# Attention kernel with two feed-forward nets: the second net's portions moved by half a unit, an eviction in three operations, and the smoothing states read earlier

## The chip, the cores and the metric

The kernel runs on one core of a Trainium2 chip. The metric is the device time of one execution in microseconds (us), as the median of several executions. The core has five engines that work side by side and meet at semaphores: TensorE (PE in the rows, with its weight loads as PEld), VectorE (DVE), ScalarE (ACT), GpSimd (POOL) and SyncE (SP), whose instructions here are DMA issues.

## The reference

Four batches of 2048 tokens with 256 features are normalised, and two blocks read the result. All is float32.

```python
xh = x[:, :, :DH]                                  # DH = 128, 8 heads of 16
x1 = layernorm(xh + mha(xh, wq1, ...), g1, be1)
xs = holt(x, 0.1, 0.1)                             # a linear recurrence over the tokens
x2 = layernorm(xs[..., :DH] + mha(xs[..., :DH], wq2, ...), g2, be2)
y = concatenate([x1, x2], -1)
attn = layernorm(y + relu(y @ w_ff1.T + b_ff1) @ w_ff2.T + b_ff2, g_ff, be_ff)
ffn = relu(x @ W1 + b1) @ W2 + b2                  # 256 -> 1024 -> 256, the "second net"
out = x_in + attn + ffn                            # x = layernorm(x_in)
```

## The kernel before

Each batch passes through three stages, and each engine has its own program in which they follow one another: a **prologue** (transposes, the smoothing of `holt`, the projections to keys, queries and values), the **attention**, and the **nets** (the first net, `w_ff`, and the output). In `middle(b)` the prologue of batch b+1 stands between the attention and the nets of batch b.

**The attention** is 16 units (`PAIRED_UNITS`: two attentions, four chunks of 512 queries, two groups of four heads). A unit has 16 key tiles, here called kts, and each kt has two steps, so `STEPS = 32`. A step is one product of keys and queries on TensorE (`scores`, line 1487) and one exponential over 128x1024 on ScalarE (line 746). The scores go to two buffers in turn, so `scores(at)` waits until exponential `at - 2` is done. A kt also has one product with the values (`values`, line 1505), which adds into two PSUM banks `o_banks` over the whole unit; the two banks hold the sums over the two halves of the keys. At the first kt of the next unit `values` waits for `o_read`, that is until VectorE has read both banks. The order of TensorE's instructions is written out by hand in `attention` (lines 1509 to 1527): in each kt two scores, then the values, and between the two scores, in kts named by lists, a piece of other work.

**That other work** is the second net, cut into 8 halves of 256 tokens for a batch (`HALVES`, index `i`). The first layer of a half is 8 portions (`second_hidden`, k = 0 to 7), the second layer 8 more (`second_out_part`; k = 0 to 3 make the first tile of 128 tokens, k = 4 to 7 the second). Before, an even unit 2i has the 8 portions of the first layer of half i, and the odd unit 2i+1 the 8 portions of its second layer. All products of a portion are 48 instructions of line 1270, written into the two PSUM banks `sides`. VectorE takes up each portion of the first layer with `hidden_half` (lines 921 to 927, four operations; `hid2_read` is counted after the second), and portion k + 1 waits for `hid2_read` of portion k. Each tile of the second layer is taken up by `second_tile` (lines 936 and 943).

**The end of a unit.** VectorE's `evict` (lines 864 to 870) reads both `o_banks`, adds them and shuffles the rows. After an odd unit the pair of groups is complete: `second_sums`, two `invert` (the reciprocal, line 887) and `attended` (lines 893 and 895) make `att`, TensorE's `out_projection` multiplies it (line 1270 too, 64 instructions into the same `sides`), and `add_projection` (lines 913 and 915) adds it to `resid`. `check_sums` (899 to 903) is a test of ranges. In the even unit these pieces stand between the first-layer portions on VectorE: `hidden_half` 0, `second_sums`, `hidden_half` 1, `invert(0)`, and so on. `out_projection` stands in kt 9, and waits for `att_ready` and for `hid2_read` of portion 4, which VectorE reads after `attended`. In some odd units VectorE has a layer norm of the next batch (`layer_norm`) or `first_y` between its two `second_tile`.

**The smoothing in the prologue of a later batch ("joint")**: TensorE makes local states, VectorE copies them (`local_states`), then each chunk's state follows from the one before (`next_state` on both engines, lines 1365 and 1026), and each smoothed chunk is finished by `carried` (line 1383). `out_projection` of the last unit follows `carried(2)`, and the transposes (`turned`, line 1337) wait for `out_read`, the end of `add_projection`.

Of the kernel before, what the change touches and what calls it, by code (L numbers as in the profile page):

```python
# [73 lines left out]
HIDDEN_KTS, OUT_KTS, PROJECTION_KT, BEFORE_PROJECTION = [0, 2, 4, 6, 8, 11, 13, 14], [0, 2, 4, 6, 8, 10, 12, 14], 9, 5  # L74
# [139 lines left out]
def build(nc, x, packed, w_ff, w_ffn, out):  # L214
# [8 lines left out]
    with ctx:  # L223
# [71 lines left out]
        def fast_programs():  # L295
# [493 lines left out]
            def vector_program(dve):  # L789
# [71 lines left out]
                def evict(b, n):  # L861
# [3 lines left out]
                    dve.tensor_copy(o_sb[:, n % 2, :], o_banks[1]).then_inc(o_read, 1)  # L865
                    hold(dve, o_read, u + 2)
                    step.settle()
                    step(dve.tensor_tensor(rden[:, :], rden[:, :], o_sb[:, n % 2, :], ALU.add))
                    step.settle()
# [134 lines left out]
                def prologue(b, before=None):  # L1004
# [88 lines left out]
                    if before is not None:  # L1093
                        evict(before, UNITS2 - 1)
                        second_sums()
                        invert(0)
                        local_states()
                        invert(1)
                        next_state(2)
                        attended(before, UNITS2 - 1)  # L1100
                        next_state(3)
                        state_read()
                        check_sums(before, UNITS2 - 1)
                        add_projection(before, UNITS2 - 1)
                        smoothed()
# [54 lines left out]
                def attention(b, next_norm):  # L1160
                    for n in range(UNITS2):
# [3 lines left out]
                        if n % 2 == 0:  # L1165
                            hidden_half(b, i, 0)
                            if n > 0:
                                second_sums()
                            hidden_half(b, i, 1)
                            if n > 0:  # L1170
                                invert(0)
                            hidden_half(b, i, 2)
                            if n > 0:
                                invert(1)
                            hidden_half(b, i, 3)
                            if n > 0:
                                attended(b, n - 1)
                            hidden_half(b, i, 4)
                            if n > 0:
                                add_projection(b, n - 1)  # L1180
                                check_sums(b, n - 1)
                            for k in range(5, HB):
                                hidden_half(b, i, k)
                        else:
# [17 lines left out]
                            second_tile(b, i, 1)  # L1202

# [1331 lines left out]
```

## Time and profile before

| | us |
|---|---|
| median of 3 executions | 2614.68 (2612.33 to 2617.86) |
| the profiled execution, device time | 2602.86 |
| its span | 2601.0 |
| TensorE (PE) busy | 2356.7 (91%) |
| ScalarE busy | 2183.9 (84%) |
| VectorE busy | 1627.0 (63%) |
| exponentials (line 746), busy | 1313.5 + 671.5 |

The span is the time between the first and the last instruction. Busy time is merged over instructions that overlap, so TensorE's 91% counts a time in which a pipelined product is still in flight as busy. The exponentials overlap their neighbours slightly too, which is why 2048 of 1.04 us each make 1985 us.

### The profile page before, as it was taken

Reading aid. Unit: us, or ns where it says so; the run is one execution under the profiler, and the core shown is the slowest. Engines: PE = TensorE matmul, PEld = TensorE weight load, DVE = VectorE, ACT = ScalarE, POOL = GpSimd, SP = SyncE. Lnnn points to the kernel's source line nnn. Section 1 sums busy time; section 2 is a strip of 40 time slices with the busy share of each in tenths; the row PEclk is TensorE's granted clock in tenths of the full one; section 3 lists DMA queues with packets and bytes.
Section 4 is the critical chain, followed back from the end, with each engine's and each line's share of the span. In section 5 each row is a group of like instructions: output and inputs, shape, how many; then the busy total and the mean of one; then the engine's idle time right before and its main releaser. Section 6 shows DMA issues by size and latency. Waiting matters only on the chain.

```text
span 2601.0 us, 134879 instructions
## 1 busy us (share of the span) xinstructions
PE 2356.7 (91%) x62849; PEld 1206.9 (46%) x62849; DVE 1627.0 (63%) x3603; ACT 2183.9 (84%) x2419; POOL 382.2 (15%) x375
## 2 busy tenths in 40 slices
PE   6899899999999989999999999999999999999995
PEld 4344444446644444445654444444565444444454
DVE  5456666667746666665775656666577565566676
ACT  5899999976499999996569999999556999999952
POOL 1100100004410020000440002000054000100053
PEclk9999999999999999998999999999899999999998
DMA  8100210005110030000610002000151000200001
GB/s 223 47 20 24 49 37 12 8 7 125 55 39 20 20 62 12 12 8 7 139 60 20 20 20 62 12 12 8 38 109 51 12 12 24 50 12 12 8 30 42
DMA packets 49946, 100.33 MB, mean 39 GB/s; under 512 B 7888, under 2 KB 32464, under 8 KB 48992
## 3 DMA queue, kind: packets, MB, share of 16 engines
q1 hardware_dynamic: 42880, 76.92, 10.8%
q0 software_dynamic: 6496, 14.69, 3.2%
q8 instruction: 494, 8.09, 1.3%
q14 instruction: 76, 0.62, 0.1%
HBM read 57.45 MB, written 34.08 MB: 35 GB/s over the span
## 4 chain that ended last, share of the span: by engine, by line
ACT 37%; PE 25%; DVE 22%; issue 14%; DMA 1%; POOL 1%; DVEq 0%; SPq 0%; ACTq 0%; POOLq 0%
ACT p_sb L746 24%; ACT area L746 12%; PE slot L1557 5%; PE slot L1505 5%; PE slot L1573 5%; DVE rden L887 4%; DVE hid_one L921 3%; PE slot L1487 2%; PE slot L1270 2%; DVE hid_one L923 2%; PE slot L1392 2%; DVE hid_parts L927 2%; DVE o_sb L893 2%; DVE hid_parts L925 1%; PE slot L1401 1%
## 5 line engine op out<-in xcount | busy, mean ns | idle before, releaser
L746 ACT ACTIVATE p_sb<-slot 128x1024 f32<-128x1024 f32 x1368 | 1313.5, 1038 | 99.9 <-PE slot L1487 88.1
L1487 PE MATMUL slot<-q_st,k_st 50*32 50x512 f16 x16384 | 840.0, 381 | 124.9 <-ACT p_sb L746 76.0
L1505 PE MATMUL slot<-p_sb,v_sb 64*17 64x512 f32 x10944 | 724.9, 593 | 0.1
L746 ACT ACTIVATE area<-slot 128x1024 f32<-128x1024 f32 x680 | 671.5, 1039 | 19.0 <-PE slot L1487 17.6
L1487 PEld LDWEIGHTS slot<-q_st,k_st 50*32 50x32 f16 x16384 | 240.3, 90 | 933.9 <-ACT p_sb L746 614.2
L936 DVE SCALAR_TENSOR_TENSOR second<-slot,second 128x256 f32<-128x256 f32 x128 | 54.3, 424 | 506.9 <-PE slot L1270 504.8
L1505 PE MATMUL slot<-area,v_sb 64*17 64x512 f32 x5440 | 358.3, 589 | 0.5 <-issue 0.5
L1270 PE MATMUL slot<-xt_parts,w_parts 64*32 64x256 f16 x12288 | 217.9, 269 | 7.9 <-issue 3.5
L1270 PE MATMUL slot<-w_parts,hid_parts 64*32 64x256 f16 x12288 | 216.5, 268 | 2.0 <-issue 1.9
L1505 PEld LDWEIGHTS slot<-p_sb,v_sb 64*17 64x17 f32 x10944 | 199.5, 94 | 35.9 <-issue 2.7
L921 DVE TENSOR_SCALAR hid_one<-slot,b_grown 128x256 f32<-128x256 f32 x256 | 123.7, 483 | 120.4 <-PE slot L1270 115.1
L1270 PEld LDWEIGHTS slot<-xt_parts,w_parts 64*32 64x32 f16 x12288 | 163.7, 92 | 67.1 <-DVE hid_one L923 36.5
L1270 PEld LDWEIGHTS slot<-w_parts,hid_parts 64*32 64x32 f16 x12288 | 173.0, 93 | 43.2 <-issue 10.1
L1573 PE MATMUL slot<-wf_parts,p_sb 128*128 128x256 f16 x1536 | 175.0, 273 | 5.3 <-POOL p_sb L620 5.3
L1557 PE MATMUL slot<-area,wf_parts 128*128 128x512 f16 x768 | 170.4, 382 | 2.5 <-DVE area L964 2.5
L600 POOL TENSOR_TENSOR resid<-resid,con 128x1024 f32<-128x1024 f32 x16 | 37.9, 2367 | 877.4 <-DVEq L954 877.4
L620 POOL TENSOR_TENSOR p_sb<-area,p_sb 128x512 f16<-128x512 f32 x128 | 149.9, 1172 | 100.0 <-ACT p_sb L762 94.0
L1573 PEld LDWEIGHTS slot<-wf_parts,p_sb 128*128 128x128 f16 x1536 | 148.9, 98 | 29.9 <-POOL p_sb L620 9.7
L443 POOL DMA_DIRECT2D k_st<-part_dram x48 | 24.4, 514 | 834.5 <-PE slot L1505 833.6
L761 ACT ACTIVATE area<-slot,bf_grown 128x512 f32<-128x512 f32 x128 | 88.0, 687 | 50.1 <-PE slot L1557 45.1
L927 DVE SCALAR_TENSOR_TENSOR hid_parts<-hid_one,hid_parts 128x256 f16<-128x256 f32 x256 | 118.5, 463 | 8.7
L887 DVE RECIPROCAL rden<-den 128x256 f32<-128x256 f32 x64 | 112.1, 1752 | 9.1 <-DVE hid_parts L927 1.0
(125 smaller groups left out, 2205.1 us busy)
## 6 DMA issues: line engine op xcount, KB each, us to landing
part_dram<-p_sb SPq DMA_DIRECT2D x16, 1024.0 KB, 4.1
xn<-x SPq DMA_DIRECT2D x16, 512.0 KB, 5.1
second<-x SPq DMA_DIRECT2D x32, 256.0 KB, 3.4
ffn_dram<-second SPq DMA_DIRECT2D x32, 256.0 KB, 2.3
area<-ffn_dram SPq DMA_DIRECT2D x16, 512.0 KB, 5.1
out<-area SPq DMA_DIRECT2D x15, 512.0 KB, 3.3
k_st<-part_dram SPq DMA_DIRECT2D x24, 256.0 KB, 11.4
k_st<-part_dram POOLq DMA_DIRECT2D x48, 128.0 KB, 3.7
```

The lines of the kernel that those rows point to most:

```text
L620: pool.tensor_tensor(h_lo[:, m, :], h_one[:, m % 2, :], h_hi[:, m, :], ALU.subtract).then_inc(hid_ready, 1)
L746: act.activation(p_ring[n % P_RING], slot[n % 2][:, :], ACT.Exp, scale=0.25 / GROW ** 2).then_inc(exp_done, 1)
L761: act.activation(h_one[:, m % 2, :], bank, ACT.Relu, bias=bf_grown[:, m:m + 1])
L887: step(dve.reciprocal(rden[:, cols], den[:, cols]))
L921: step(dve.tensor_scalar(hid_one[:, :], sides[0][:, cols], b1_grown[:, k:k + 1], None, ALU.add))
L927: dve.scalar_tensor_tensor(hid_lo[:, k, :], hid_one[:, :], 0.0, hid_hi[:, k, :], ALU.max, ALU.subtract).then_inc(hid2_ready, 1)
L936: out = dve.scalar_tensor_tensor(tile, sides[r][:, t * D:(t + 1) * D], 1.0 / (X_GROW * W_GROW * W_GROW), tile, ALU.mult, ALU.add)
L1270: mm = pe.matmul(sides[r][ROW * j:ROW * (j + 1), cols], lhs[rows_, ROW * j:ROW * (j + 1)], rhs[rows_, :], start=start, stop=stop, skip_gro ...
L1487: mm = pe.matmul(slot[n][ROW * r:ROW * (r + 1), k * CHUNK:(k + 1) * CHUNK], k_st[rows_, pair, kt * P + ROW * r:kt * P + ROW * (r + 1)], q_ ...
L1505: mm = pe.matmul(o_banks[r][ROW * j:ROW * j + DK + 1, :], v_sb[rows_, a, kt, GH * g + j, :], p_ring[n % P_RING][rows_, (j % 2) * CHUNK:(j ...
L1557: mm = pe.matmul(slot[m // 2 % 2][:, (m % 2) * CHUNK:(m % 2 + 1) * CHUNK], w[:, k, m * P:(m + 1) * P], src[:, k * CHUNK:(k + 1) * CHUNK], ...
L1573: mm = pe.matmul(bank[:, t * D:(t + 1) * D], src[:, m, t * P:(t + 1) * P], w[:, m, :], start=(m == 0 and r == 0), stop=(m == HB - 1 and r ...
```

## The change

The portions are placed anew, half of each layer in each unit. An even unit has the last four portions of the first layer (`HIDDEN_LATE`, kts 0, 2, 4, 6), the projection in kt 10 and the first four portions of the second layer (`OUT_EARLY`, kts 12 to 15). An odd unit has the last four of the second layer (`OUT_LATE`, kts 3, 4, 6, 7) and the first four of the next half's first layer (`HIDDEN_EARLY`, kts 9, 11, 13, 14). Unit 0 is as before; unit 1 has twelve portions. VectorE's order follows. `evict` has three operations for four: the second bank is added straight from PSUM, after the first has been copied. In the joint prologue `local_states` comes ahead of `invert(0)`, and `attended` after `state_read`.

```diff
-HIDDEN_KTS, OUT_KTS, PROJECTION_KT, BEFORE_PROJECTION = [0, 2, 4, 6, 8, 11, 13, 14], [0, 2, 4, 6, 8, 10, 12, 14], 9, 5
+HIDDEN_LATE, PROJECTION_KT, OUT_EARLY = [0, 2, 4, 6], 10, [12, 13, 14, 15]
+OUT_LATE, HIDDEN_EARLY = [3, 4, 6, 7], [9, 11, 13, 14]
+ALL_OUT, HIDDEN_NEXT = [0, 1, 2, 3, 5, 6, 7, 8], [10, 11, 13, 14]
@@ evict
                     step(dve.tensor_copy(rden[:, :], o_banks[0]))
-                    dve.tensor_copy(o_sb[:, n % 2, :], o_banks[1]).then_inc(o_read, 1)
+                    step.settle()
+                    dve.tensor_tensor(rden[:, :], o_banks[1], rden[:, :], ALU.add).then_inc(o_read, 1)
                     hold(dve, o_read, u + 2)
-                    step.settle()
-                    step(dve.tensor_tensor(rden[:, :], rden[:, :], o_sb[:, n % 2, :], ALU.add))
-                    step.settle()
@@ prologue of VectorE
                         second_sums()
+                        local_states()
                         invert(0)
-                        local_states()
+                        next_state(2)
                         invert(1)
-                        next_state(2)
-                        attended(before, UNITS2 - 1)
                         next_state(3)
                         state_read()
+                        attended(before, UNITS2 - 1)
@@ attention of VectorE, even units after 0
                             hidden_half(b, i, 4)
+                            second_sums()
+                            hidden_half(b, i, 5)
+                            invert(0)
+                            hidden_half(b, i, 6)
+                            invert(1)
+                            hidden_half(b, i, 7)
+                            attended(b, n - 1)
+                            add_projection(b, n - 1)
+                            check_sums(b, n - 1)
@@ odd units
                             second_tile(b, i, 1)
+                            if i + 1 < HALVES:
+                                for k in range(HB // 2):
+                                    hidden_half(b, i + 1, k)
@@ out_projection of TensorE
-                        pe.wait_ge(hid2_read, HB * (HALVES * b + i) + BEFORE_PROJECTION)
+                        pe.wait_ge(hid2_read, HB * (HALVES * b + i + 1))
@@ second_hidden
-                    if k == BEFORE_PROJECTION and i > 0:
-                        pe.wait_ge(out_read, CHUNKS2 * b + i)
-                    elif k > 0:
+                    if k > 0:
@@ second_out_part
                     if k == 0:
                         pe.wait_ge(hid2_read, HB * (h + 1))
+                        if i > 0:
+                            pe.wait_ge(out_read, CHUNKS2 * b + i)
```

## Rows read from the trace of the kernel before

**Rows 1.** The page: busy time by engine, and the chain that ended last
```profile
PE 2356.7 (91%) x62849; PEld 1206.9 (46%) x62849; DVE 1627.0 (63%) x3603; ACT 2183.9 (84%) x2419; POOL 382.2 (15%) x375
...
ACT 37%; PE 25%; DVE 22%; issue 14%; DMA 1%; POOL 1%; DVEq 0%; SPq 0%; ACTq 0%; POOLq 0%
```
**Rows 2.** Windows: an even unit, an odd unit, batch 1's attention (busy, granted clock)
```profile
132.81:165.01 32.20, 28.66 (x968) 13.46 (x960) 25.57 (x50) 29.84 (x33) 0.00 (x0) 1.00 0.11 37
165.01:194.62 29.61, 27.62 (x904) 12.78 (x896) 11.91 (x40) 29.58 (x33) 0.00 (x0) 1.00 0.02 4
...
704.20:1201.20 497.00, 453.08 (x14760) 209.99 (x14752) 296.47 (x727) 476.13 (x512) 41.23 (x50) 0.99 0.09 24
```
**Rows 3.** Timeline of ScalarE in the even unit (start, us, idle before)
```profile
140.50 3.93 ACT L746 ACTIVATE p_sb<-slot 128x1024 f32<-128x1024 f32 x4 [0.19 <-PE slot L1487]
...
155.68 2.10 ACT L746 ACTIVATE p_sb<-slot 128x1024 f32<-128x1024 f32 x2 [2.06 <-PE slot L1487]
157.68 1.94 ACT L746 ACTIVATE area<-slot 128x1024 f32<-128x1024 f32 x2
159.48 3.79 ACT L746 ACTIVATE p_sb<-slot 128x1024 f32<-128x1024 f32 x4
```
**Rows 4.** Waits over the whole span: total us, times, longest
```profile
PEld slot L1270 <- DVE att L895: 58.1, 26, 2.5
```
**Rows 5.** Timeline of TensorE around the projection of that unit
```profile
152.12 0.40 PE L1487 MATMUL slot<-q_st,k_st 50*32 50x512 f16 x8
154.27 1.13 PE L1270 MATMUL slot<-con,att 64*32 64x128 f32 x63 [1.76 <-DVE hid_one L923]
```
**Rows 6.** Timeline of VectorE in the same unit
```profile
135.41 0.69 DVE L864 COPY rden<-slot 128x512 f32<-128x512 f32 x1 [1.54 <-PE slot L1505]
136.02 0.68 DVE L865 COPY o_sb<-slot 128x512 f32<-128x512 f32 x1
136.85 0.69 DVE L868 TENSOR_TENSOR rden<-rden,o_sb 128x512 f32<-128x512 f32 x1
...
152.52 0.75 DVE L895 SCALAR_TENSOR_TENSOR att<-o_sb,con 128x512 f32<-128x512 f32 x1
153.19 0.48 DVE L921 TENSOR_SCALAR hid_one<-slot,b_grown 128x256 f32<-128x256 f32 x1
153.70 0.42 DVE L923 TENSOR_TENSOR hid_one<-slot,hid_one 128x256 f32<-128x256 f32 x1
...
155.55 0.69 DVE L913 TENSOR_TENSOR resid<-slot,resid 128x512 f32<-128x512 f32 x1 [0.64 <-PE slot L1270]
156.28 0.69 DVE L915 TENSOR_TENSOR resid<-slot,resid 128x512 f32<-128x512 f32 x1
```
**Rows 7.** Timeline of TensorE in an odd unit: one kt with a portion
```profile
182.12 0.40 PE L1487 MATMUL slot<-q_st,k_st 50*32 50x512 f16 x8
182.34 0.84 PE L1270 MATMUL slot<-w_parts,hid_parts 64*32 64x256 f16 x48
183.00 0.40 PE L1487 MATMUL slot<-q_st,k_st 50*32 50x512 f16 x8
183.22 1.04 PE L1505 MATMUL slot<-area,v_sb 64*17 64x512 f32 x16
184.08 0.40 PE L1487 MATMUL slot<-q_st,k_st 50*32 50x512 f16 x8
```
**Rows 8.** Timeline of ScalarE in unit 0 of batch 0
```profile
84.12 3.82 ACT L746 ACTIVATE p_sb<-slot 128x1024 f32<-128x1024 f32 x4
...
93.43 1.96 ACT L746 ACTIVATE area<-slot 128x1024 f32<-128x1024 f32 x2
95.70 3.93 ACT L746 ACTIVATE p_sb<-slot 128x1024 f32<-128x1024 f32 x4 [0.31 <-PE slot L1487]
```
**Rows 9.** Timeline of VectorE in the odd unit
```profile
167.60 0.69 DVE L864 COPY rden<-slot 128x512 f32<-128x512 f32 x1 [1.11 <-PE slot L1505]
...
171.33 0.49 DVE L876 TENSOR_SCALAR den<-den,con 128x512 f32<-128x512 f32 x1
```
**Rows 10.** Timeline of TensorE after batch 0's attention
```profile
577.07 0.37 PE L1365 MATMUL slot<-state,con 2*2 2x128 f32 x2 [1.90 <-DVE state L1022]
...
583.01 1.16 PE L1270 MATMUL slot<-con,att 64*32 64x128 f32 x64
```
**Rows 11.** Windows between two attentions, batches 0, 1 and 2
```profile
568.10:704.20 136.10, 131.99 (x968) 89.76 (x960) 102.69 (x175) 66.53 (x90) 52.65 (x40) 1.00 0.36 85
1201.20:1344.60 143.40, 139.83 (x968) 94.82 (x960) 102.74 (x175) 66.82 (x91) 52.66 (x40) 0.94 0.35 81
1841.50:1983.30 141.80, 138.24 (x968) 93.77 (x960) 102.74 (x175) 66.79 (x92) 52.66 (x40) 0.95 0.35 82
```

More of the change, by code:

```diff
@@ L1164, in attention @@
                             evict(b, n - 1)
[L1165 to L1177, printed above, removed]
-                            hidden_half(b, i, 4)
[L1179 to L1183, printed above, removed]
+                        if n == 0:
+                            for k in range(HB):
+                                hidden_half(b, 0, k)
+                        elif n % 2 == 0:
+                            hidden_half(b, i, 4)
+                            second_sums()
[7 more added lines that the diff above has]
+                            check_sums(b, n - 1)
                         else:
@@ L1513, in attention @@
                     for unit in range(UNITS2):
-                        net_kts = OUT_KTS if unit % 2 else HIDDEN_KTS if unit else FIRST_HIDDEN_KTS
+                        i = unit // 2
                         for kt in range(TILES):
@@ L1519, in attention @@
                                 scores(made)
-                            if kt in net_kts:
-                                (second_out_part if unit % 2 else second_hidden)(b, unit // 2, net_kts.index(kt))
-                            if kt == PROJECTION_KT and unit > 0 and unit % 2 == 0:
-                                out_projection(b, unit - 1)
+                            if unit == 0:
+                                if kt in FIRST_HIDDEN_KTS:
+                                    second_hidden(b, 0, FIRST_HIDDEN_KTS.index(kt))
+                            elif unit == 1:
+                                if kt in ALL_OUT:
+                                    second_out_part(b, 0, ALL_OUT.index(kt))
+                                if kt in HIDDEN_NEXT:
+                                    second_hidden(b, 1, HIDDEN_NEXT.index(kt))
+                            elif unit % 2 == 0:
+                                if kt in HIDDEN_LATE:
+                                    second_hidden(b, i, HB // 2 + HIDDEN_LATE.index(kt))
+                                if kt == PROJECTION_KT:
+                                    out_projection(b, unit - 1)
+                                if kt in OUT_EARLY:
+                                    second_out_part(b, i, OUT_EARLY.index(kt))
+                            else:
+                                if kt in OUT_LATE:
+                                    second_out_part(b, i, HB // 2 + OUT_LATE.index(kt))
+                                if kt in HIDDEN_EARLY and i + 1 < HALVES:
+                                    second_hidden(b, i + 1, HIDDEN_EARLY.index(kt))
                             for at in range(made + 1, ahead):
```

## The prediction

> **What bounds the kernel now.** I began with the shares of the page [rows 1]: TensorE is busy for 91% of the span and ScalarE for 84%, yet the chain that ended last runs most through ScalarE (37%), so busy shares alone do not name the bound. The windows by unit do [rows 2]. Batch 1's attention takes 497.0 us, in which ScalarE is busy for 476.1, so it idles for only 21 us; four attentions are about 1986 of the 2601 us. Inside, an odd unit takes 29.61 us with ScalarE busy for 29.58. An even unit takes 32.20 with 29.84 busy. The attention is thus bound by ScalarE's exponentials in odd units, and in even units something holds ScalarE for 2.4 us.
>
> The timeline of ScalarE says where [rows 3]: 2.06 us ahead of the exponential at 155.68 and 0.19 at 140.50, both released by scores. From 157.68 to 159.48 two steps take 1.80 us: the free pace is about 0.905 us a step, or 28.96 for the 32 of a unit. TensorE's timeline has the cause [rows 5]: scores at 152.12, free again 0.22 later, and then nothing until the projection at 154.27, which by TensorE's fixed order stands ahead of the next scores. It waits for VectorE, first for `att` (line 895) and then for `hid_one` (line 923), the read of portion 4: VectorE has `att` ready at 153.27 and that read at 154.12 [rows 6]. The waits show the pattern is general: 58 us in 26 waits on `att` [rows 4]. There are 7 such even units in a batch (units 2 to 14), 28 in all.
>
> **The change, part by part.**
>
> *The projection in kt 10, behind portions 4 to 7 alone.* Two things happen to what it waits for. The read of the fifth portion no longer stands behind `attended`, so `att` (0.85 us earlier) is the last to come. And the eviction is shorter: now the copies start at 135.41 and 136.02 and the add at 136.85, ending at 137.54 [rows 6]. The new add reads PSUM and SBUF like line 913, 0.69 us, and cannot overlap the first copy: 135.41 + 0.69 + 0.05 + 0.69 = 136.84. VectorE saves 0.70 us, and all behind it up to `att`, which was back to back, comes at 152.57 in place of 153.27. The projection stood to start at 152.34 (152.12 + 0.22); one kt later is 1.81 more, 154.15. So `att` is 1.6 us early, where the release was 1.9 us late. The 2.06 us wait should go whole, and the 0.19 us wait too (portion 1 waited for VectorE's read of portion 0, itself behind the eviction). That is 2.25 us an even unit.
>
> *What is late next.* The first portion of the second layer, in kt 12, now waits for `out_read`. From the projection's start to the end of line 915 are 156.97 - 154.27 = 2.7 us [rows 5, 6]; from the projection in kt 10 to the portion in kt 12 are 2 x 1.81 = 3.6. It is covered with 0.9 us to spare. In the odd unit portion 4 of the second layer, now in kt 3, waits for `second_tile(0)`. VectorE's eviction starts at 167.60 and the work behind it ends at 171.82 [rows 9], 0.7 earlier now, and two reads of 0.42 end at about 172.1; a portion in kt 3 starts about 8.1 us after the unit's first exponential, 173.1. One us to spare, less up to 0.5 for a unit that begins later.
>
> *What the new places cost.* One kt with a portion is, by starts [rows 7], 0.22 (scores) + 0.66 (portion) + 0.22 (scores) + 0.86 (values) = 1.96 us of TensorE, against 1.81 for two exponentials; one without is 1.30. A portion alone is made good in the next kt, and leaves 0.08 us: the odd unit with eight takes 29.61 - 28.96 = 0.65. Each further portion in a row costs 1.96 - 1.81 = 0.15. The same count gives the old even unit: five alone 0.40, one more 0.08, a pair 0.23, the projection about 0.2, the two waits 2.25: 28.96 + 3.16 = 32.12, against 32.20 read. For the new even unit: four alone 0.32, the four in kts 12 to 15 0.53, projection 0.2, so 30.0. For the new odd unit: three pairs 0.69, two alone 0.16, so 29.8, and 0.2 for its start, because the portion in kt 15 delays the last values and the new `o_read` comes 0.14 later than the copy's did, so that the next values wait. Together 60.0 against 61.8 before: 1.8 us a pair. These small costs partly hide one another, since any kt without a portion has 0.5 us to spare and resets TensorE; followed kt by kt with the same durations, the pair comes to 59.6. I take 59.8: 2.0 us x 28 = **56 us**. Unit 1 of each batch takes twelve portions: two runs of four and two pairs, 28.96 + 1.52 = 30.5 for 29.6, so 4 x 0.9 = **3.5 us back**. Unit 15, with four portions fewer, gains about what its start costs.
>
> Unit 0 bounds the cost of portions in a row: it has pairs in kts 6, 7 and 9, 10 and a row of three in 12 to 14. From 84.12 to 93.43 are ten steps in 9.31 us, 0.26 over the free pace; then the row of three makes one of 0.31 idle [rows 8]. A row of four second-layer portions, which need no read between them, lies between 0.5 and 1.0.
>
> *The joint prologue.* After batch 0's attention TensorE stood 1.90 us for VectorE's copy of the states, which was behind `invert(0)` [rows 10]; with `local_states` 1.75 (the reciprocal) and 0.70 (the eviction) earlier, the copy is done before TensorE asks. The projection at 583.01 could then start 1.9 us earlier. But `attended` is now behind `next_state(3)`, which TensorE's chain feeds: `att` comes at about 581.5, and `check_sums` still stands ahead of `add_projection`, so the transposes start about 0.95 us earlier. 3 x 0.95 = **3 us**. The bounds are 0 (if `att` is the later) and 1.9 each. Nothing is moved on the queues of SP and POOL: their loads are released by counts that come no later.
>
> *The clock.* Between attentions the granted clock is 1.00 after batch 0, 0.94 and 0.95 after batches 1 and 2, at the same work and the same 1.9 us stand, and these stretches last 136.1, 143.4 and 141.8 us [rows 11]: half clock costs 7.3 and 5.7. The stand that precedes the fall goes, but one stretch had it without a fall. I take one of the two as gone, **6.5 us**; the bounds are 13 gained (both) and 7 lost (batch 0's falls as well). The Trainium skill, "TensorE: Matmul & The Clock Gate", Part 1, says the gate sets the clock by how busy TensorE has lately been. By it both stretches would go, and the sum would be 6.5 us better; batch 0's stretch, with the same stand at full clock, doesn't bear it out as it stands.
>
> Sum: 56 - 3.5 + 3 + 6.5 = 62 us. The profiled execution took 2602.9 us, and would become 2540.9. The median of the runs is 11.8 us above it; the saving is taken from the median: 2614.7 - 62 = **2552.7**, I say 2553.
>
> **The rivals.**
>
> *A new wait in place of the old (2580).* The chain on VectorE slips past one of the two new waits. For: TensorE's order is fixed, so each us that `out_read` or `second_tile(0)` is late costs ScalarE 1 us in every pair, and the margins are 0.9 us and 0.5 to 1. Against: the rows above. A slip that leaves 1 us of wait gives 28 us less, 2553 + 28 = 2581.
>
> *The stall only moves (2601).* If the release is not `att` but follows the projection by a kt, the even unit keeps its 2.06 us; what is left is the prologue, the clock and 0.2 us a unit: 14 us at most. Against: in the rows `att` follows VectorE's own back-to-back work, not TensorE.
>
> *TensorE is the bound, slower than before (2640).* The page has TensorE at 91% [rows 1], and 28.66 of 32.20 us in the even unit [rows 2]. If a portion that has another one just ahead costs its full 0.66 us rather than 0.15, then the six such of a pair of units (three in kts 12 to 15, one in each of three pairs) cost 6 x 0.51 = 3.1 us more, against the 2.0 gained: 28 x 1.1 = 31 us slower, with unit 1's eight such 16 us more, less the 9.5 of prologue and clock, about 2640 to 2650. It decides from 0.15 + 2.0 / 6 = 0.5 us for each. For it speaks only the busy share; against it, unit 0, where two pairs cost 0.26 us in all. The Trainium skill, "Perfetto Trace Analysis", Identifying the Most-Contended Engine, also warns that matmul busy share is no measure of how near TensorE is to its limit, because its work is pipelined; the weight loads' share in these rows is 46%, which goes with that.
>
> **How the numbers follow.** The forecast has a chance of 0.64, its own range 2535 to 2568 (clock 6.5 either way, pairs 59.6 to 60.1, prologue 0 to 1.9). A new wait has 0.22, the stall that only moves 0.07, TensorE as the bound 0.05; 0.02 is left for causes that I don't see. The range has to take in the forecast and most of the new wait: 2532 to 2585. Faster by over 0.2%, which is about what a measurement of this kernel can tell from no change: 0.94, slower 0.05, within 0.01.
>
> **What the changed profile would show.** Even units near 30.0 us, odd ones too, with no idle of ScalarE of 2 us; the projection right behind its scores, not released by `att` or `hid_one`; three VectorE operations to an eviction, about 2.2 us. Portions in a row of four should start 1.96 us apart. After the attention the second line 1365 should follow line 1377 without a stand. The prediction fails if waits of `out_read` (line 915) or line 936 appear ahead of line 1270, if the four portions start further than 2.3 us apart, or if the clock falls after each of three attentions.

## The result and the profile after

| us | before | after |
|---|---|---|
| median of the runs | 2616.3 (4 runs) | 2590.3 (4 runs) |
| ratio | | 0.9901 (0.988 to 0.9921) |
| span of the profiled execution | 2601.0 | 2587.9 |
| attention of batches 0 to 3 | 496.6, 497.0, 496.9, 494.9 | 496.0, 498.6, 496.7, 495.5 |
| between two attentions | 136.1, 143.4, 141.8 | 135.4, 135.3, 135.3 |

The change makes the kernel 1.0% faster, 26 us, where 62 us were forecast. The table has the two surprises: the attention, which was to give 52 of them, gave nothing (1985.4 us in all before, 1986.8 after), and the gain lies between the attentions: 421.3 us there before, 406.0 after, 15.3 less. The span is 13.1 shorter; the attentions take back 1.4 of the 15.3, the stretches ahead of and behind them the last 0.8.

The page of the kernel after has ScalarE's idle time before its exponentials hardly changed, 92.0 + 16.5 us for 99.9 + 19.0:

```profile
PE 2374.6 (92%) x62849; PEld 1220.9 (47%) x62849; DVE 1614.7 (62%) x3539; ACT 2194.7 (85%) x2419; POOL 382.2 (15%) x375
...
PE 45%; ACT 37%; issue 13%; DVE 2%; POOL 1%; DMA 1%; SPq 0%; DVEq 0%; ACTq 0%; POOLq 0%
...
L748 ACT ACTIVATE p_sb<-slot 128x1024 f32<-128x1024 f32 x1368 | 1318.8, 1037 | 92.0 <-PE slot L1485 80.0
```

In the chain VectorE went from 22% to 2% and TensorE from 25% to 45% [rows 1]: the waits for VectorE are gone, and TensorE holds the end instead. Lines 1485, 1503 and 1268 are what 1487, 1505 and 1270 were, and line 748 what 746 was. The windows of an even unit, of the odd one behind it and of unit 1 (after; us, then busy time of TensorE, its loads, VectorE, ScalarE, GpSimd, and the granted clock):

```profile
1080.10:1110.00 29.90, 27.87 (x920) 12.99 (x912) 20.27 (x37) 29.82 (x34) 0.00 (x0) 1.00 0.02 4
1110.00:1141.20 31.20, 28.36 (x952) 13.30 (x944) 19.07 (x62) 29.68 (x33) 4.76 (x2) 1.00 0.04 13
...
738.00:769.70 31.70, 30.83 (x1093) 15.92 (x1080) 12.77 (x30) 30.04 (x33) 0.87 (x1) 1.00 0.13 38
```

This even unit takes 29.90 us for 32.20 [rows 2], about the 30.0 of the forecast. The odd one right behind it takes 31.20 for 29.61, and unit 1 has gone from 29.6 to 32.4 (median of the four batches; the one shown took 31.70). Only three of the seven even units (4, 12 and 14) have a median of 29.9; the other four are at 30.7 to 31.0. Taking for each of a batch's sixteen units the median over the four batches, units 2 to 14 (even) gain 12.4 us together, units 3 to 13 (odd) lose 9.2, unit 1 loses 2.8 and unit 15 1.0: nothing is left.

Where an odd unit loses, TensorE stands with no semaphore to wait for. Its timeline (after) and, in its critical form, the chain through the same place:

```profile
1110.73 0.84 PE L1268 MATMUL slot<-w_parts,hid_parts 64*32 64x256 f16 x48
1111.39 0.40 PE L1485 MATMUL slot<-q_st,k_st 50*32 50x512 f16 x8
1112.70 1.08 PE L1503 MATMUL slot<-p_sb,v_sb 64*17 64x512 f32 x16 [0.91 <-issue]
```
```profile
1110.92 0.66 PE slot L1268 x48
1111.57 0.22 PE slot L1485 x8
1111.79 0.91 issue
1112.70 1.08 PE slot L1503 x16
1113.78 0.24 PE slot L1485 x8
```

The first weight load of that group of values had started at 1111.39; the second came at 1112.70. "Issue" is time in which the engine waited for nothing that the profile shows. ScalarE pays for it with 1.12 us at 1114.04:

```profile
1111.91 1.02 ACT L748 ACTIVATE area<-slot 128x1024 f32<-128x1024 f32 x1
1114.04 1.02 ACT L748 ACTIVATE area<-slot 128x1024 f32<-128x1024 f32 x1 [1.12 <-PE slot L1485]
```

This is no single event. The waits of weight loads with the releaser issue, in the kernel before and then in the one after (us in total, times, longest):

```profile
PEld slot L1270 <- issue: 22.0, 49, 2.1
PEld slot L1487 <- issue: 17.6, 47, 3.7
PEld slot L1505 <- issue: 5.3, 10, 1.4
```
```profile
PEld slot L1268 <- issue: 41.8, 111, 1.9
PEld slot L1503 <- issue: 37.4, 72, 1.8
PEld slot L1485 <- issue: 36.8, 102, 2.9
```

To count it in one number I call it a **stand** when two weight loads of one group, between which the program has no wait, start more than 0.25 us apart, and count those in the attentions, by the starts in the trace. Before has 20 stands, 15.4 us in all; after has 85, 64.5 us. These counts are not exact: a wider count, in which the recorded waits alone divide the loads, has 24 pairs (18.6 us) before and 139 (89.7 us) after with the same threshold. What hardly depends on the way of counting is the number of pairs more than 0.5 us apart: 15 (15.1 us) before, 72 (65.3 us) after.

**What arrives before a stand ends.** Instructions come by a DMA queue of their own. The page has 494 packets of 8.09 MB, both before and after, so 16 KB each, which I call blocks; with 2 x 62849 products and loads of TensorE that makes about 254 instructions a block. The DMA view of 1106 to 1116 us (after), in slices of 0.25 us:

```profile
GB/s 66 0 0 0 0 0 0 0 0 0 0 0 0 0 0 0 0 66 0 0 0 0 0 0 0 0 0 0 0 0 0 66 0 0 0 0 0 0 0 0
...
q8 instruction: 3, 0.05, 2.0%
```

A block's transfer starts in the slice at 1110.25 (by its record at 1110.37, ending at 1111.32), and 1.38 us after that end TensorE goes on. Counted over the whole kernel, not the attentions alone, there are 89 stands, and at 84 of them a block arrived in this way: the median from a block's arrival to TensorE's next start is 1.43 us (nine in ten between 1.25 and 1.58), and from the start of the transfer 2.6 us. Of the 72 pairs over 0.5 us apart in the attentions, 71 end 1.2 to 1.65 us after a block has arrived; such stretches make up about a tenth of the attentions, so by chance it would be 7. Between the start of the transfer and the stand TensorE has started 148 instructions (median). So my theory, an estimate from these numbers: TensorE's stock when a block is ordered lasts about 150 instructions, the block is usable after 2.3 to 2.9 us, and a stretch faster than about 60 instructions per us for that long runs dry. A kt with a portion has 64 + 96 = 160 instructions, in 1.96 us 82 per us; a kt without has 64. One portion in two kts is 224 in 3.62 us, 62 per us: just at the limit.

### The profile page after: what moved, and what is told of

Same layout as the page of the kernel before. It is cut to its first block, busy times and chain, and to the rows that moved or that the text cites. A ratio compares the mean times of both kernels' runs of the same rounds, so it can differ in the third digit from the quotient of the medians.

```text
span 2587.9 us, 134790 instructions
## 1 busy us (share of the span) xinstructions
PE 2374.6 (92%) x62849; PEld 1220.9 (47%) x62849; DVE 1614.7 (62%) x3539; ACT 2194.7 (85%) x2419; POOL 382.2 (15%) x375
## 3 DMA queue, kind: packets, MB, share of 16 engines
q8 instruction: 494, 8.09, 1.3%
## 4 chain that ended last, share of the span: by engine, by line
PE 45%; ACT 37%; issue 13%; DVE 2%; POOL 1%; DMA 1%; SPq 0%; DVEq 0%; ACTq 0%; POOLq 0%
ACT p_sb L748 24%; PE slot L1503 14%; ACT area L748 11%; PE slot L1485 8%; PE slot L1268 7%; PE slot L1571 5%; PE slot L1587 5%; PE slot L1390 2%; POOL p_sb L622 1%; PE slot L1399 1%; PE slot L1335 1%; ACT area L763 1%; PE slot L1352 1%; ACT p_sb L764 1%; PE slot L1375 1%
## 5 line engine op out<-in xcount | busy, mean ns | idle before, releaser
L1485 PE MATMUL slot<-q_st,k_st 50*32 50x512 f16 x16384 | 876.1, 382 | 128.7 <-ACT p_sb L748 76.9
L1503 PE MATMUL slot<-p_sb,v_sb 64*17 64x512 f32 x10944 | 756.9, 593 | 4.2 <-issue 2.3
L748 ACT ACTIVATE area<-slot 128x1024 f32<-128x1024 f32 x680 | 675.0, 1038 | 16.5 <-PE slot L1485 13.9
L1485 PEld LDWEIGHTS slot<-q_st,k_st 50*32 50x32 f16 x16384 | 255.1, 90 | 916.6 <-ACT p_sb L748 580.7
L1503 PE MATMUL slot<-area,v_sb 64*17 64x512 f32 x5440 | 373.2, 590 | 2.5 <-issue 2.3
L1268 PE MATMUL slot<-w_parts,hid_parts 64*32 64x256 f16 x12288 | 227.7, 269 | 14.0 <-issue 13.9
L866 DVE COPY rden<-slot 128x512 f32<-128x512 f32 x64 | 44.3, 692 | 314.2 <-PE slot L1503 314.2
L1503 PEld LDWEIGHTS slot<-p_sb,v_sb 64*17 64x17 f32 x10944 | 205.8, 93 | 67.7 <-issue 24.5
L1268 PEld LDWEIGHTS slot<-w_parts,hid_parts 64*32 64x32 f16 x12288 | 178.9, 92 | 66.5 <-issue 39.2
L1268 PEld LDWEIGHTS slot<-xt_parts,w_parts 64*32 64x32 f16 x12288 | 169.7, 92 | 50.0 <-DVE hid_one L923 20.2
```

The lines of the kernel that those rows point to most:

```text
L748: act.activation(p_ring[n % P_RING], slot[n % 2][:, :], ACT.Exp, scale=0.25 / GROW ** 2).then_inc(exp_done, 1)
L1268: mm = pe.matmul(sides[r][ROW * j:ROW * (j + 1), cols], lhs[rows_, ROW * j:ROW * (j + 1)], rhs[rows_, :], start=start, stop=stop, skip_gro ...
L1485: mm = pe.matmul(slot[n][ROW * r:ROW * (r + 1), k * CHUNK:(k + 1) * CHUNK], k_st[rows_, pair, kt * P + ROW * r:kt * P + ROW * (r + 1)], q_ ...
L1503: mm = pe.matmul(o_banks[r][ROW * j:ROW * j + DK + 1, :], v_sb[rows_, a, kt, GH * g + j, :], p_ring[n % P_RING][rows_, (j % 2) * CHUNK:(j ...
```

## The experiments

Ratios are to the kernel before, run beside each; where only a profile was taken it is said. The expectations are quoted; A, B and C are the theories named in them.

**The states read at once, alone.**

```diff
                         second_sums()
+                        local_states()
                         invert(0)
-                        local_states()
+                        next_state(2)
                         invert(1)
-                        next_state(2)
-                        attended(before, UNITS2 - 1)
                         next_state(3)
                         state_read()
+                        attended(before, UNITS2 - 1)
```

> The kernel before with only the new order of the joint prologue on VectorE (local_states ahead of invert(0), attended after state_read); portions and eviction as before. Theory A (the whole profiled gain of the change, 13 us, lies between the attentions, because TensorE's stand of 1.9 us goes and the clock no longer falls there): each of the three stretches between attentions about 135.4 us at granted clock 1.00, span about 2587 to 2589, and the attentions stay at 496 to 497 us. Rival (the clock falls by chance, and what changed is the moment at which the stretch begins): the stretches get only 0.5 to 1.9 us shorter each, one or two of them still at 0.94 to 0.95, span 2596 to 2600.

Measured: ratio 0.9921 (0.9904 to 0.9937). The stretches between attentions took 135.5, 136.8 and 135.5 us; the attentions varied, 498.3, 494.1, 501.7 and 498.2. The stretches of 143.4 and 141.8 us are gone; what is left of the fall is a short one of 3.4 us in the second stretch. The span, 2594.0, is above the forecast 2587 to 2589, because the attentions came out 6.9 us longer in all than in the profile of before.

**The eviction in three operations, alone** (the diff of `evict` above).

> The kernel before with only the eviction in three operations. Theory A (the stall of 2.06 us of an even unit follows VectorE's chain): the wait ahead of the exponential at step 22 shrinks by 0.6 to 0.7 us to about 1.4 in each of 28 even units, and the one at step 8 goes; attention of a batch about 491 us, span about 2577 to 2582. Rival (o_read 0.14 us later than the copy's costs the next values, in every one of 64 units): the gain is eaten up, attention 496 us.

Measured: ratio 0.9893 (0.9865 to 0.992), attentions 492.8, 492.8, 495.6 and 493.3. The even units are at 31.6 us for 32.2, which is 0.6 each and 17 us in the 28; the odd ones stay at 29.6. Part of the forecast held (the wait shrinks, the later `o_read` costs nothing), but of the 17 us the attentions show only 11, with unit 0 and unit 7 longer. The rest of its gain is again between attentions: 141.3, 135.6 and 135.9. TensorE's stand there shrinks from 1.90 us to 1.32, and in two of three stretches the clock did not fall.

**The portions alone** (the changed kernel with the old `evict` and the old order in the prologue).

> The changed kernel with the old eviction and the old order in the joint prologue: only the portions and the projection are moved. Theory A (the attention of the changed kernel gains 2 us in each even unit and loses it in odd units and units 1 and 7, because TensorE's instructions come too late where portions stand close together): attention 496 to 499 us a batch as in the changed kernel, idle of TensorE with the releaser issue inside the groups of the values and the portions, 80 to 90 stands over 0.25 us, 60 to 75 us in all; span 2597 to 2605. Rival (the longer odd units come from the later o_read, that is from the eviction in three operations): attention 490 us or less and the odd units at 29.8.

Measured: ratio 1.0014 (1.0002 to 1.0026), no faster. Attentions 501.1, 500.8, 502.7 and 497.3; 89 stands, 72.5 us. Between attentions 141.7, 143.3 and 143.4. The stands are as many as forecast; the span, 2620.7, is 16 us above the forecast range, with three attentions over 500. The odd units 3 to 13 are at 30.6 to 31.5 here too (unit 7 at 32.6), without the new eviction, so the later `o_read` is not what lengthens them.

**The changed kernel with a quarter of the instructions in each portion.**

```diff
-                    for j in range(P // ROW):
-                        for r in range(2):
-                            rows_ = slice(HALF * r, HALF * (r + 1))
-                            mm = pe.matmul(sides[r][ROW * j:ROW * (j + 1), cols], lhs[rows_, ROW * j:ROW * (j + 1)], rhs[rows_, :],
+                    for r in range(2):
+                        rows_ = slice(HALF * r, HALF * (r + 1))
+                        mm = pe.matmul(sides[r][:, cols], lhs[rows_, :], rhs[rows_, :],
... (start, stop and skip_group_check as before)
```

> The changed kernel with side_product in 2 products over 64 rows and all 128 columns in place of 8 over 64 rows and 32 columns each: the same sums with a quarter of the instructions (a portion has 12 products with their weight loads, not 48; the projection 16, not 64). Theory A (TensorE runs dry of instructions where portions stand close together; instructions come in blocks of 16 KB and a stand ends about 1.4 us after such a block has arrived): the stands inside the groups go, odd and even units come to 29.9 or less, attention 478 to 484 us, span about 2530. Rival B (TensorE's own work is too much, its arrays being busy): the same work in fewer instructions takes the same time, attention 496 to 499. Rival C (a change of tile shape between portions and scores costs on its own, or the weight load of 128 columns is not hidden): a portion takes over 0.8 us rather than 0.66, attention over 500.

Measured: ratio 1.0013 (0.9999 to 1.0027), attentions 504.1, 504.1, 501.7 and 502.9. The stands fall from 85 to 2 (0.8 us), and yet it is slower than the changed kernel. Two timelines of TensorE, the wide portion and, above in [rows 7], the narrow one, have the reason:

```profile
171.44 0.40 PE L1484 MATMUL slot<-q_st,k_st 50*32 50x512 f16 x8
171.77 0.83 PE L1267 MATMUL slot<-w_parts,hid_parts 64*128 64x256 f16 x12
172.53 0.41 PE L1484 MATMUL slot<-q_st,k_st 50*32 50x512 f16 x8
172.75 1.04 PE L1502 MATMUL slot<-area,v_sb 64*17 64x512 f32 x16
173.62 0.88 PE L1484 MATMUL slot<-q_st,k_st 50*32 50x512 f16 x16
```

From the scores to the portion 0.33 us for 0.22, from the portion to the next scores 0.76 for 0.66, so a kt with a portion takes 2.18 us rather than 1.96. Every unit from 2 to 14 is at 31.3 us, evenly. Of theory A the stands came true and the time (478 to 484 us an attention) did not; of rival C the time came true, over 500, though the portion grew less than it said (0.76 us to the next scores, not over 0.8). The 0.11 us at each change between narrow and wide tiles outweighs the stands. Whether it is the change of shape or the longer weight loads of 128 columns this run does not separate. It also tells what regular work near the limit looks like beside starved work: all units alike, against 29.9 and 31.2 in turn.

**The cause doubled: more instructions for the same columns** (one profile).

```diff
-                        for r in range(P // ROW):
-                            for k in range(2):
...
+                        for s_ in range(2):
+                            for r in range(P // ROW):
+                                for k in range(2):
+                                    rows_, lo = slice(HALF * k, HALF * k + ROWS), s_ * CHUNK // 2
+                                    mm = pe.matmul(slot[n][ROW * r:ROW * (r + 1), k * CHUNK + lo:k * CHUNK + lo + CHUNK // 2],
... (weights as before, 256 of the 512 columns of q_st)
```

> The kernel before with each scores product of 512 columns split in two of 256: the same columns through TensorE, 512 more instructions in a unit (1792 becomes 2304 for eight portions, scores and values). Theory A (instructions arrive in blocks of 256, and TensorE stands when it has used up its stock before the next block is there; a block took 2.3 to 2.9 us from the start of its transfer until use): hundreds of stands over 0.25 us inside the groups (before: 20 in the attentions), most ending 1.3 to 1.6 us after a block has landed, attention 520 us or more a batch. Rival (the stands of the changed kernel come from the arrays or the memories, not from the count of instructions): 20 to 40 stands, attention within 2% of 497 us.

Measured: 2844.7 us, attentions 554.7, 556.4, 552.1 and 555.2: 58 us more a batch. 265 stands, 218.4 us; of 339 pairs of loads more than 0.5 us apart, 322 end 1.2 to 1.65 us after a block has arrived. The waits (us, times, longest):

```profile
PEld slot L1488 <- issue: 287.1, 833, 3.9
PEld slot L1270 <- issue: 107.8, 180, 2.4
PEld slot L1507 <- issue: 102.0, 112, 1.6
```

The page has 622 blocks for 494: 128 more for the 32768 instructions more, 256 for each block, so this queue does carry TensorE's instructions. The time follows the count of instructions, not the columns. The rival, that the arrays or the memories were the limit, is out. There is another, a fixed cost of each extra product, and the timeline of TensorE settles it:

```profile
187.70 0.41 PE L1488 MATMUL slot<-q_st,k_st 50*32 50x256 f16 x16
187.93 0.84 PE L1270 MATMUL slot<-w_parts,hid_parts 64*32 64x256 f16 x48
...
191.66 0.40 PE L1488 MATMUL slot<-q_st,k_st 50*32 50x256 f16 x16
191.88 0.71 PE L1270 MATMUL slot<-w_parts,hid_parts 64*32 64x256 f16 x34
192.76 0.41 PE L1270 MATMUL slot<-w_parts,hid_parts 64*32 64x256 f16 x14 [0.17 <-issue]
```

From the start of the sixteen half products to the portion are 0.23 and 0.22 us, as for the eight whole ones [rows 7], and so it is at the median of all 463 such places (0.22). While its instructions are there, TensorE does the split scores in the same time; what the run costs more is lost in stands, like the one inside the second portion.

**Both parts without moved portions.** The kernel before with the new `evict` and the new prologue.

> The kernel before with the eviction in three operations and the states read at once, and no portion moved. Theory A (these two parts make the whole gain of the change, and the portions cost 5 to 15 us of it): attention about 493 us a batch as with the eviction alone, the stretches between attentions 135.5 us at full clock, span 2570 to 2576, ratio to the kernel before 0.982 to 0.985, faster than the changed kernel by 0.5 to 0.8%. Rival (the parts overlap, both only shorten the stand after the attention): ratio 0.988 to 0.990, the same as each alone.

Measured: ratio 0.9853 (0.9828 to 0.9877); attentions 494.9, 495.3, 498.5 and 494.8; between them 135.3, 137.2 and 135.3. It is about 0.5% faster than the changed kernel: moving the portions cost 9 us by the medians, which come from two sessions. The product of the two ratios is 0.981; that both had the clock's gain in them would explain the shortfall, but given the intervals it is hardly clear of noise.

**Another placement: projection in kt 10.** To that kernel:

```diff
-HIDDEN_KTS, OUT_KTS, PROJECTION_KT, BEFORE_PROJECTION = [0, 2, 4, 6, 8, 11, 13, 14], [0, 2, 4, 6, 8, 10, 12, 14], 9, 5
+HIDDEN_KTS, OUT_KTS, PROJECTION_KT, BEFORE_PROJECTION = [0, 2, 4, 6, 8, 12, 13, 15], [1, 3, 5, 7, 9, 11, 13, 14], 10, 5
```

> As the one with both parts, and the projection in kt 10 without moving portions by half a unit: first-layer portions in kts 0, 2, 4, 6, 8, 12, 13, 15 of even units, second-layer ones in 1, 3, 5, 7, 9, 11, 13, 14 of odd units, so that there are two places at most with portions in neighbouring kts in a unit. Theory A (instructions run dry only where portions stand close together): the idle of 1.4 us ahead of the projection goes without stands elsewhere, even units 30.0 to 30.5, odd 29.6 to 29.9, attention 480 to 486 us, span 2530 to 2550. Rival (any projection between portions without a wait uses up the stock of instructions, since its 64 products come on top of eight portions): stands of TensorE inside groups rise from 20 to over 50, even units 31, attention 488 to 492.

Measured: ratio 0.985 (0.9829 to 0.9871), attentions 493.2, 490.8, 493.5 and 496.1 for a forecast 480 to 486, with 32 stands of 22.7 us. Even units are at 29.9 to 31.9, but the odd ones rose to 30.9, and not by stands. The waits name a cause that the expectation had not (us, times, longest):

```profile
PEld slot L1503 <- DVE rden L866: 24.9, 28, 1.0
...
PE slot L1503 <- DVE rden L866: 16.6, 28, 0.7
```

The portion in kt 15 delays the unit's last values, VectorE reads `o_banks` later, and the first values of the next unit wait for line 866: 24.9 us in 28 units by the weight loads. The 16.6 us of the products are the same 28 waits, seen from TensorE's other row.

**The same with a wide projection only.**

> As the spread one, with the projection alone in products of 64 rows by 128 columns (16 products rather than 64). Theory A: 96 instructions fewer in each even unit, against one change of tile shape of about 0.2 us; stands inside groups no more than in the spread one, even units within 0.2 us of it, span within 0.3% of it. Rival (the stock of instructions is short in the whole unit, not only where portions are close): even units 0.3 to 0.8 us shorter than in the spread one.

Measured: 0.9854 (0.9829 to 0.9878), no difference; stands 28, 15.4 us for 22.7.

**Six portions ahead of the projection.** To the kernel with both parts:

```diff
-HIDDEN_KTS, OUT_KTS, PROJECTION_KT, BEFORE_PROJECTION = [0, 2, 4, 6, 8, 11, 13, 14], [0, 2, 4, 6, 8, 10, 12, 14], 9, 5
+HIDDEN_KTS, OUT_KTS, PROJECTION_KT, BEFORE_PROJECTION = [0, 2, 4, 6, 8, 10, 13, 14], [0, 2, 4, 6, 8, 10, 12, 14], 11, 6
@@ VectorE, even units
                             hidden_half(b, i, 4)
+                            hidden_half(b, i, 5)
                             if n > 0:
                                 add_projection(b, n - 1)
                                 check_sums(b, n - 1)
-                            for k in range(5, HB):
+                            for k in range(6, HB):
                                 hidden_half(b, i, k)
```
The order of the eviction and of the prologue is as in the kernel with both parts.

> As the one with both parts, with six first-layer portions ahead of the projection and the projection in kt 11: portions in kts 0, 2, 4, 6, 8, 10, 13, 14 of even units, odd units as before. Theory A (a place is free if TensorE waits for nobody there and is not left without instructions): the wait of 1.4 us ahead of the projection goes, the odd units stay at 29.6 since nothing stands in kt 15, and kts 10 to 14 with 736 instructions in 9 us leave some stands in even units: even units 30.0 to 30.6, attention 482 to 488 us, span 2535 to 2555, ratio 0.972 to 0.980. Rival (every placement without the wait comes out at 490 to 496 us because the blocks of instructions set the average too): odd units rise over 30 and stands over 50.

Measured: **2539.6 us, ratio 0.9714 (0.9694 to 0.9733)**. Attentions 483.6, 484.2, 482.9 and 481.7. Even units 29.9 to 31.1, odd ones 29.6 (30.0 and 30.4 in units 5 and 7), 41 stands of 25.1 us. It beats the kernel before by 73 us and, by the medians of two sessions, the changed one by 51. No portion is in kt 15, nothing waits for VectorE at the projection, and only kts 10 to 14 of even units go fast through instructions. The windows of an even and an odd unit of it:

```profile
132.00:164.00 32.00, 29.89 (x976) 14.08 (x961) 23.35 (x44) 30.41 (x34) 0.00 (x0) 1.00 0.12 37
1128.50:1158.10 29.60, 28.06 (x952) 13.24 (x943) 21.82 (x42) 29.36 (x33) 0.00 (x0) 1.00 0.02 4
```

The first is one of its worst, with two waits of ScalarE that add up to 1.55 us (the stretch is cut at round numbers, and the second straddles the two units):

```profile
144.34 2.86 ACT L746 ACTIVATE p_sb<-slot 128x1024 f32<-128x1024 f32 x3 [0.66 <-PE slot L1486]
...
160.93 3.93 ACT L746 ACTIVATE p_sb<-slot 128x1024 f32<-128x1024 f32 x4 [0.89 <-PE slot L1486]
```

**The same with a wide projection.**

> The same with the projection alone in products of 64 rows by 128 columns, 96 instructions fewer in an even unit. Theory A: fewer stands than in the one with the late projection, even units 0 to 0.4 us shorter, span 0 to 10 us less. Rival (the change of tile shape costs as much as the stands): no difference beyond 3 us.

Measured: 0.9717 (0.9698 to 0.9736). Stands fall to 21 (14.5 us), the time does not: the rival, the change of shape costs what the stands did.

**Both kernels profiled once more.**

> The kernel before, unchanged, profiled once more. Theory A (the clock falls after the attentions whenever TensorE stands 1.9 us there, most of the time, and the first profile with one of three stretches at full clock was a lucky one): two or three of the three stretches at 141 to 143.5 us, attentions 495 to 500 us, 15 to 25 stands inside groups, span 2600 to 2616. Rival (the profiled executions differ in the attentions, not the clock): attentions of over 500 us and stretches at 136.

Measured: span 2622.3 us, above the forecast 2600 to 2616; all three stretches at half clock for 17 us each (granted clock 0.94), attentions 498.7, 498.3, 499.6 and 500.3, 31 stands for a forecast 15 to 25:

```profile
570.50:713.90 143.40, 139.87 (x968) 94.84 (x960) 102.76 (x174) 66.79 (x91) 52.61 (x40) 0.94 0.36 81
1212.20:1355.60 143.40, 139.83 (x968) 94.75 (x960) 102.77 (x174) 66.97 (x91) 52.60 (x40) 0.94 0.34 81
1855.20:1998.60 143.40, 139.77 (x968) 93.94 (x952) 102.75 (x174) 66.82 (x91) 52.61 (x40) 0.94 0.34 81
```

> The changed kernel, unchanged, profiled once more. Theory A: stretches between attentions 135 to 137 us, attentions 494 to 500 us, 75 to 95 stands inside groups, the even units with no stand at 29.9 us, span 2585 to 2595. Rival (the stands of the first profile were of one execution): fewer than 50 stands, attentions 485 to 490 us.

Measured: span 2606.0; stretches 137.4, 137.2 and 135.3, attentions 500.7, 501.3, 502.5 and 497.0, 94 stands of 74.5 us. The stretches are 20.3 us shorter than in the kernel before beside it, and the attentions 4.7 longer together: the same account as in the first pair, so neither rival stands. Both spans and most attentions of this pair are longer than was expected, in both kernels alike, and why is open. The span gains 16.3 us here and 13.1 in the first pair, in which the kernel before had one stretch at full clock. That stretch accounts for some 7 us; why the medians differ by 26 is in part open.

## Why the prediction was right or wrong

**The wait at the projection: right.** `att` came early enough; the waits for line 895 that are left belong to the prologues of the next batch (4.4 us in 3 times), and the three even units (4, 12, 14) whose median is free of stands take 29.90 us against 30.0 by my count. The eviction took 2.34 us (VectorE's timeline, after) for 2.2:

```profile
1082.65 0.69 DVE L866 COPY rden<-slot 128x512 f32<-128x512 f32 x1 [1.11 <-PE slot L1503]
1083.37 0.69 DVE L868 TENSOR_TENSOR rden<-slot,rden 128x512 f32<-128x512 f32 x1
1084.22 0.01 DVE L870 LOAD_MASK_SELECT o_sb<-rden  x1 [0.15 <-DVE rden L868]
1084.24 0.75 DVE L870 STREAM_SHUFFLE o_sb<-rden 128x512 f32<-128x512 f32 x1
```

**What the new places cost: wrong, and this is the step that failed.** I had priced a further portion in a row at 0.15 us, from starts inside single kts [rows 7] and from unit 0 [rows 8]. The arithmetic of those starts is right as long as TensorE has instructions: in the even units' row of four the portions did start 1.96 us apart (median of 66 distances; 7 are over the 2.3 that I had named as a sign of being wrong). But TensorE does not always have them. The attentions took 85 stands of 64.5 us, most of them with or just behind portions in neighbouring kts: over a quarter of the 139 pairs of the wider count lie in the first two kts of odd units, behind the row of four. A pair of an even and an odd unit takes 61.7 us by the medians, where I had 59.8; spread over its six further portions, that makes about 0.43 us each instead of 0.15 (an estimate), and unit 1, at 32.4 for my 30.5, gives 0.39 in the same way. The first two terms of the sum, 56 - 3.5 = 52.5 us gained in the attentions, measured as a loss of 1.4 us in the first pair of profiles and of 4.7 in the second. The portions alone cost 0.14%, where by my count they were to be the main gain.

**The sign was in the trace of before.** The waits of weight loads with the releaser issue were there, 45 us in 106 times, and I had read only those that name an engine. So was the odd idle time in units 7, 8 and 9, which had no explanation in my account. And the idle of 0.31 us in unit 0, which I took as the price of three portions in a row, was itself a stand. TensorE's timeline of before, just ahead of that exponential:

```profile
94.66 0.39 PE L1487 MATMUL slot<-q_st,k_st 50*32 50x512 f16 x5
95.26 0.39 PE L1487 MATMUL slot<-q_st,k_st 50*32 50x512 f16 x3 [0.21 <-issue]
```

The eight products of one scores group, which has no wait inside it, break off after five, and go on 1.27 us after a block's transfer ended (93.99 by its record). The row that I used as a bound held the mechanism that broke the forecast.

**The rivals.** "TensorE is the bound" had the right engine and the wrong resource: neither its columns nor the share in the page, but how fast its instructions arrive. Its price was near, too: it needed about 0.5 us for each further portion to make the change a loss, and 0.43 was measured. Without the other two parts the moved portions are 0.14% slower than before. The new waits on `out_read` and `second_tile` did not come. The stall that only moves did not either.

**The joint prologue: right in mechanism.** TensorE no longer stands for the states; `att` is now the late one, and the transposes wait for line 915, as forecast (timeline, after):

```profile
575.58 0.37 PE L1363 MATMUL slot<-state,con 2*2 2x128 f32 x2
...
582.23 1.16 PE L1268 MATMUL slot<-con,att 64*32 64x128 f32 x64 [0.64 <-DVE att L895]
...
585.47 0.76 PE L1335 MATMUL slot<-con,xn 128*128 128x128 f32 x5 [1.03 <-DVE resid L915]
```

In the kernel before the same step had stood 1.90 us [rows 10]. From the last exponential to the transposes are 16.9 us for 17.7, 0.8 gained for a forecast 0.95.

**The clock: undersized.** I had taken 6.5 us for one stretch. Both of the profile's went (15.3 us with the prologue's), and with all three falling, as in the second profile, it is 20 (prologue included). The rule of the Trainium skill ("TensorE: Matmul & The Clock Gate", Part 1), that the gate follows how busy TensorE has lately been, gave the better number here: by it both stretches would go. Over the profiles, the stretch between two attentions had a full fall, 13.7 or 17.1 us at half clock and 141.3 us or more in length, in 11 of 12 cases with the 1.9 us of standing (the kernel before twice, the portions alone, and the run with doubled instructions); in 1 of 3 with 1.3 us of standing (the eviction alone); and in none of 27 with the states read at once, though short falls of 3.4 to 6.8 us remain in 11 of these.

**The margin of the median.** I took the saving from the median though the profile lay 12 us below it, and called the two alike. They differed in part by the very thing at issue, one stretch of half clock.

## What to carry to other kernels

In a program written out in line, with many small products, TensorE's instructions are a resource of their own: count products and weight loads per us in the densest stretches of a plan, not only busy time, and read the waits whose releaser is "issue" as a warning before adding to such places. When a placement is moved, look at which place is free of every shared thing at once: the wait on another engine, the last kt of a unit on which the next unit's eviction hangs, and the flow of instructions. And where half clock comes and goes, ask of a small idle time ahead of it what it costs in all, since 1.9 us of standing was worth up to 7.3.

## What the runs showed of the hardware

- TensorE's instructions arrived in blocks of 16 KB, about 254 products and loads (128 blocks more for 32768 instructions more in the doubled run); one was used 1.25 to 1.58 us after its transfer ended (84 stands), 2.6 us after it started. The Trainium skill, "Runtime: NRT & Kernel Launch", Instruction fetch mechanics, has the same blocks of 16 KiB, and says that fetching is hidden because the sequencer issues more slowly than the blocks arrive. The blocks agree; that it is hidden does not hold here: 96 instructions of a portion were issued in 0.66 us [rows 7], and 64.5 us of stands followed from it.
- Going from tiles of 64x32 to 64x128 and back cost about 0.11 us each way (0.33 us for 0.22, 0.76 for 0.66), the longer weight loads included.
- Splitting the products of 512 columns into two cost 58 us in an attention of 497, with no column more; where TensorE had its instructions, the split group still took 0.22 us.
- With a stand shortened from 1.90 to 1.32 us the clock stayed up in two of the three stretches of one profile, so a gain measured in a prologue may be the clock's.
